# One transfer per expert, and gathers that skip empty rows, in a routed-expert kernel

## What is computed

```python
h = tok_ref(x, W, b, g1, b1, g2, b2)       # layer norm, 1024 -> 512, layer norm
h = h + attn_ref(layernorm(h), w_gate, g_gate, w_down, g_down)   # quantised gated MLP, width 1408
h = h + ffn_ref(layernorm(h), router_w, w_gate, w_up, w_down)

def ffn_ref(x, router_w, w_gate, w_up, w_down):     # 32 experts, 8 for each token, width 192
    probs = softmax(x @ router_w.T)
    rw, sel = top_k(probs, 8)
    rw = rw / sum(rw)
    for e in range(32):
        w_e = sum(where(sel == e, rw, 0))
        acc += (silu(x @ wg[e]) * (x @ wu[e])) @ wd[e] * w_e[:, None]
```

## Time and profile before

| | |
|---|---|
| median of 3 runs | 308.67 us (306.58 to 308.88) |
| profiled execution | 307.58 us |
| its span | 305.8 us |
| first gather issued | 103.33 us |
| first tile's rows turned | 107.06 us |
| last tile's down product ends | 279.7 us |
| last scatter issued | 283.06 us |
| mean DMA rate over the span | 280 GB/s |
| mean granted TensorE clock | 0.977 of full speed |

### The profile page before, as it was taken

How to read it: one execution, slowest core, us unless ns; L and a number is a source line. 1 busy time by engine, 2 the same in 40 slices (tenths; PEclk the granted TensorE clock), 3 DMA queues, 4 the chain that set the end, 5 groups by cost and what they waited for, 6 DMA issues and landing times.

```text
span 305.8 us, 3907 instructions
## 1 busy us (share of the span) xinstructions
PE 279.5 (91%) x1159; PEld 147.4 (48%) x1159; DVE 151.0 (49%) x446; ACT 125.1 (41%) x213; POOL 126.4 (41%) x130
## 2 busy tenths in 40 slices
PE   4899999779999889999999999999989999949991
PEld 1435444455557355655465556555645554533231
DVE  2648999995988523343523333323323322303364
ACT  2347998999974221332133213321322232211101
POOL 4062211976521422246435643464355446443310
PEclk9999999999998699999999999999999999997997
DMA  7999999503998298799999999999999999974883
GB/s 251 332 424 417 381 405 309 189 0 120 336 316 281 52 294 292 259 269 331 341 316 313 352 327 313 323 327 312 310 342 335 301 316 337 324 171 65 162 217 124
DMA packets 27798, 85.51 MB, mean 280 GB/s; under 512 B 4209, under 2 KB 4337, under 8 KB 26785
## 3 DMA queue, kind: packets, MB, share of 16 engines
q1 hardware_dynamic: 19760, 64.78, 61.0%
q0 software_dynamic: 7488, 18.42, 25.2%
q10 hardware_dynamic: 530, 2.08, 2.6%
HBM read 72.34 MB, written 12.92 MB: 279 GB/s over the span
## 4 chain that ended last, share of the span: by engine, by line
PE 39%; DVE 18%; DMA 17%; issue 8%; POOL 4%; ACT 3%; POOLq 0%; DVEq 0%; ACTq 0%
PE ps L1163 17%; DMA scrap<-token_rows,idx 9%; PE ps L1192 7%; DMA sum<-w_t,add_idx 5%; PE ps L1184 4%; PE ps L1195 4%; DMA ring<-sum 3%; DVE big L1443 2%; POOL sum L647 2%; DVE stats L1327 2%; PE ps L1050 2%; DVE raw L1449 2%; PE ps L1217 1%; PE ps L1147 1%; DVE hit L1625 1%
## 5 line engine op out<-in xcount | busy, mean ns | idle before, releaser
L633 POOL DMA_INDIRECT scrap<-token_rows,idx x36 | 35.9, 996 | 83.2 <-DVE idx L1628 46.8
L647 POOL DMA_INDIRECT sum<-w_t,add_idx x32 | 51.3, 1604 | 28.1 <-issue 11.5
L866 ACT ACTIVATE w_t<-ps 128x512 f32<-128x512 f32 x36 | 21.4, 597 | 85.0 <-PE ps L1184 84.8
L1644 DVE COPY w_t<-ps 128x256 f32<-128x256 f32 x34 | 14.4, 425 | 58.8 <-PE ps L1220 45.5
L1639 DVE SCALAR_TENSOR_TENSOR w_t<-ps,scrap,w_t 128x192 f32<-128x192 f32 x32 | 13.2, 413 | 57.1 <-issue 47.3
L871 ACT ACTIVATE w_t<-ps 128x192 f32<-128x192 f32 x34 | 11.2, 330 | 55.9 <-PE ps L1163 50.7
L1163 PE MATMUL ps<-ring,w_t 128*128 128x384 f32 x96 | 33.1, 487 | 0.7 <-ACT w_t L866 0.7
L1184 PE MATMUL ps<-ident,scrap 128*128 128x128 f32 x144 | 24.2, 292 | 10.1 <-DMA scrap<-token_rows,idx 6.6
L555 POOL TENSOR_TENSOR root_out<-root_in,minus_half 112x1 f32<-112x1 f32 x20 | 13.1, 654 | 46.3 <-DVE root_in L1344 46.2
L954 PE MATMUL ps<-raw,last 128*112 128x512 f32 x64 | 31.1, 639 | 0.0
L1163 PE MATMUL ps<-big,w_t 128*128 128x384 f32 x88 | 30.2, 486 | 0.0
(11 more groups left out here) (214 smaller groups left out, 470.6 us busy)
## 6 DMA issues: line engine op xcount, KB each, us to landing
big<-in_ffn_gate_up SPq DMA_DIRECT2D x15, 768.0 KB
ring<-in_ffn_gate_up SPq DMA_DIRECT2D x13, 768.0 KB
raw<-in_ffn_gate_up SPq DMA_DIRECT2D x6, 768.0 KB
last<-in_ffn_gate_up SPq DMA_DIRECT2D x6, 768.0 KB
big<-in_ffn_w_down SPq DMA_DIRECT2D x15, 256.0 KB
ring<-in_ffn_w_down SPq DMA_DIRECT2D x13, 256.0 KB
big<-in_mlp_w_in SPq DMA_DIRECT2D x2, 1536.0 KB, 17.7
big<-in_mlp_w_in SPq DMA_DIRECT2D x2, 1280.0 KB, 20.2
```

What stands on the lines that cost most here:

```text
L633: nc.gpsimd.indirect_dma_start(got[:, got_at(s), :], None, rows_dram[:, :], bass.IndirectOffsetOnAxis(ap=idx[:, s:s + 1], axis=0)).then_in ...
L647: nc.gpsimd.indirect_dma_start(acc_dram[m.two][:, :], bass.IndirectOffsetOnAxis(ap=add_idx[:, m.eight:m.eight + 1], axis=0), y[:, m.four, ...
L866: nc.scalar.activation(x_t[:, m.two, :, :], bank(2 + m.two).rearrange("p (c t) -> p c t", c=4), ACT.Copy).then_inc(xt_ready, 1)
L1644: nc.vector.tensor_copy(h_t[:, m.two, :, :], bank(6)[:, 0:2 * P].rearrange("p (c t) -> p c t", c=2)).then_inc(ht_ready, 1)
```

## The change

1. The weights of an expert come from one DRAM tensor `ffn` of 128 rows of 2560 numbers: gate and up, down rows 0 to 127, and in the last 512 columns the down rest. For even experts these columns hold the rest of the expert itself in partitions 0 to 63 and that of the next expert in 64 to 127. So an even expert is one transfer of 2560 columns, and an odd one a transfer of 2048 columns; `down_two` takes the rest of both from the even slot (`pair_rest_of`).
2. As an even slot holds something of both tiles, its load waits for the down products of both, and an odd slot's for its own; the separate wait on gate-up goes. `ld_dn` is gone: PE waits for `ld_gu` alone. The lists' loads keep a second, small transfer (`ld_rest`).
3. The tokens now are rows 0 to 447 of the DRAM tensors, and the spare rows 448 to 575. An empty place gets row 448 + p. All gathers but the first eight have a bound of 447: row numbers over it are skipped, and the buffer keeps what it held. Scatters still add 128 rows.
4. Experts 10 and 11 are still loaded after the first turned rows.

```diff
-    def down_loaded(self, u):
-        return 32 * self.k + 32 * ((NE + 4 * self.i + u) // R + 1)
+    def rest_loaded(self):
+        return 16 * self.k + 16
...
+        def pair_rest_of(n):
+
+            return slots[n - n % 2][rest_rows(n), WG + D:WCOLS]
...
-            def load_gate_up(e, n):
-                sp.dma_start(slots[n][:, 0:WG], we_gate_up[e, :, :]).then_inc(ld_gu[n], 16)
-
-            def load_down(e, n):
-                sp.dma_start(down_of(n), we_down[e, 0:P, :]).then_inc(ld_dn[n], 16)
-                sp.dma_start(down_rest_of(n), we_down[e, P:IE, :]).then_inc(ld_dn[n], 16)
-
             def load_expert(t):
-                load_gate_up(t, t)
-                load_down(t, t)
+
+                n, cols = t % R, WCOLS if t % 2 == 0 else WG + D
+                sp.dma_start(slots[n][:, 0:cols], ffn[t, :, 0:cols]).then_inc(ld_gu[n], 16)
+
+            def load_picked(e, n):
+
+                sp.dma_start(slots[n][:, 0:WG + D], ffn[e, :, 0:WG + D]).then_inc(ld_gu[n], 16)
+                sp.dma_start(down_rest_of(n), ffn[e, 0:IB, WG + D:WCOLS]).then_inc(ld_rest[n], 16)
...
             for t in range(R, NE):
-                sp.wait_ge(gu_done, t - R + 1)
-                load_gate_up(t, t % R)
-                sp.wait_ge(y_done, t - R + 1)
-                load_down(t, t % R)
+                sp.wait_ge(y_done, t - R + (1 if t % 2 else 2))
+                load_expert(t)
...
-                    sp.wait_ge(gu_done, R * k + (NE - R + n + 1))
-                    load_gate_up(bass.ds(e, 1), s)
                     sp.wait_ge(y_done, R * k + (NE - R + n + 1))
-                    load_down(bass.ds(e, 1), s)
+                    load_picked(bass.ds(e, 1), s)
...
-                nc.gpsimd.indirect_dma_start(got[:, got_at(s), :], None, rows_dram[:, :],
-                                             bass.IndirectOffsetOnAxis(ap=idx[:, s:s + 1], axis=0)
-                                             ).then_inc(ld_got[s], 16)
+                rows_ = bass.IndirectOffsetOnAxis(ap=idx[:, s:s + 1], axis=0)
+                if isinstance(m, Tile) and m.t < 8:
+                    nc.gpsimd.indirect_dma_start(got[:, got_at(s), :], None, rows_dram[:, :], rows_).then_inc(ld_got[s], 16)
+                else:
+                    nc.gpsimd.indirect_dma_start(got[:, got_at(s), :], None, rows_dram[:, :], rows_, bounds_check=TOK - 1,
+                                                 oob_is_err=False).then_inc(ld_got[s], 16)
...
                 for m in (Tile(t), Tile(t + 1)):
                     pe.wait_ge(ht_ready, m.upto())
-                    pe.wait_ge(ld_dn[m.slot], 2 * m.loaded())
...
-                nc.vector.tensor_scalar(idx[:, s:s + 1], idx_f[:, s:s + 1], iota_p[:, 0:1], None, ALU.max).then_inc(idx_ready, 1)
+                nc.vector.tensor_scalar(idx[:, s:s + 1], idx_f[:, s:s + 1], no_row[:, 0:1], None, ALU.add).then_inc(idx_ready, 1)
```

More of the change, by code:

```diff
@@ L104, in pairs_of, with program @@
         yield k, n_pairs
-def program(nc, x, w_tok, vecs, gb1, w_in, w_down, g_down, w_router, we_gate_up, we_down, out):
+def program(nc, x, w_tok, vecs, gb1, w_in, w_down, g_down, w_router, ffn, out):
     rows_dram = nc.dram_tensor("token_rows", (ROWS, ROW), F32).ap()
@@ L240, in program @@
         token = sb("token", [128, TOK], F16)
-        iota_p = sb("iota_p", [128, 1], F32)
+        no_row = sb("no_row", [128, 1], F32)
         iota_p2 = sb("iota_p2", [128, 1], F32)
@@ L315, in program @@
         ld_gu = [sem(f"ld_gu{n}") for n in range(R)]
-        ld_dn = [sem(f"ld_dn{n}") for n in range(R)]
+        ld_rest = [sem(f"ld_rest{n}") for n in range(R)]
         ld_got = [sem(f"ld_got{n}") for n in range(8)]
@@ L420, in program @@
         x_v = x.rearrange("(p g) k -> p g k", g=NG)
-        rows_v = rows_dram[P:ROWS, :].rearrange("(p g) r -> p g r", g=NG)
-        acc_v = [acc[P:ROWS, :].rearrange("(p g) d -> p g d", g=NG) for acc in acc_dram]
+        rows_v = rows_dram[0:TOK, :].rearrange("(p g) r -> p g r", g=NG)
+        acc_v = [acc[0:TOK, :].rearrange("(p g) d -> p g d", g=NG) for acc in acc_dram]
         def bcast(v, n):
@@ L460, in _ @@
             sp.wait_ge(consts, 1)
[L461 removed]
+            sp.dma_start(rows_dram[TOK:ROWS, :], zeros[:, :]).then_inc(rows_out, 16)
             for n in range(2):
[L463 removed]
+                sp.dma_start(acc_dram[n][TOK:ROWS, :], zeros[:, 0:D]).then_inc(sums_ready, 16)
             for n in range(2):
                 for g in range(NG):
[L466 to L477 removed]
+                    sp.dma_start(acc_dram[n][g * G:(g + 1) * G, :], zeros[0:G, 0:D]).then_inc(sums_ready, 16)
+            def load_expert(t):
+                n, cols = t % R, WCOLS if t % 2 == 0 else WG + D
[3 more added lines that the diff above has]
+                sp.dma_start(down_rest_of(n), ffn[e, 0:IB, WG + D:WCOLS]).then_inc(ld_rest[n], 16)
             sp.wait_ge(t1_done, NG)
@@ L584, in routing_consts @@
                 for t, pattern, base, mult in ((iota_e, [[0, 1]], 0, 1), (iota_e16, [[0, 1]], 0, 1), (iota_t, [[1, NL]], 0, 0),
-                                               (token, [[1, NG], [NG, G]], P, 0),
-                                               (iota_p, [[0, 1]], 0, 1), (iota_p2, [[0, 1]], 0, 2)):
+                                               (token, [[1, NG], [NG, G]], -TOK, -1),
+                                               (no_row, [[0, 1]], TOK, 1), (iota_p2, [[0, 1]], 0, 2)):
                     nc.gpsimd.iota(t[:, :], pattern=pattern, base=base, channel_multiplier=mult,
@@ L1194, in down_two @@
                     rows_ = rest_rows(m.slot)
-                    nc.tensor.matmul(bank(4 + m.two), h_t[rows_, m.two, 1, :], down_rest_of(m.slot), start=False, stop=True
+                    nc.tensor.matmul(bank(4 + m.two), h_t[rows_, m.two, 1, :], pair_rest_of(m.slot), start=False, stop=True
                                      ).then_inc(y_done, 1)
@@ L1206, in down_lists @@
                         if c == 0:
-                            pe.wait_ge(ld_dn[n], m.down_loaded(u))
+                            pe.wait_ge(ld_rest[n], m.rest_loaded())
                             nc.tensor.matmul(bank(4 + m.two)[rows_, :], h_t[:, m.two, 0, rows_], down_of(n), start=True, stop=False)
@@ L1765, in laid_out @@
     import numpy as np
+    rest = np.zeros((NE, P, D), we_down.dtype)
+    rest[:, 0:IB] = we_down[:, P:IE]
+    rest[0::2, IB:P] = we_down[1::2, P:IE]
     return {
@@ L1775, in laid_out @@
         "in_router_w": w_router.T.reshape(DC, 128, NE).transpose(1, 0, 2).reshape(128, DC * NE),
-        "in_ffn_gate_up": np.concatenate([w.reshape(NE, P, 4 * IE) for w in (we_gate, we_up)], axis=2),
-        "in_ffn_w_down": we_down,
+        "in_ffn": np.concatenate([w.reshape(NE, P, 4 * IE) for w in (we_gate, we_up)] + [we_down[:, 0:P], rest], axis=2),
     }
```

## The result

The changed kernel took 317.17 us (median of 4 runs, 314.41 to 317.86) against 307.62 (306.16 to 308.88) for the kernel before beside it. The ratio is 1.0295, 95% interval 1.0209 to 1.0382: 3% slower, where 302.1 us was forecast. The profiled execution took 317.86 us with a span of 315.9.

A forecast was written before the change was run, and what follows sets the result against it. PE, busy 91% of the span, was taken as the bound, so only its waits and the tail counted: list gather 3.4 + clock 1.4 + earlier waits 1.0 + tail 0.8 = 6.6 us, from 308.67 to 302.1; range 299.5 to 307.2.

The forecast's parts named there:

- The scatter in the stream: Expert stage: a scatter issued while weights stream takes 7.5 us, between 9.22 and 5.41.
- 93% forecast for the two queues: DMA queues, 170 to 190 us: weights 54% plus gathers and scatters 39%, against 105.5% before.
- 418 GB/s for the new rows: Weight stream: the new long rows flow at 418 GB/s while busy, against 348 for the old mix.
- The share of 54%: Weight queue q1, 170 to 190 us: busy share falls from 63.5% to 54%.
- The rival of the long packets: Expert stage: long weight packets lengthen scatters to 10.8 us, pairs to 11.7, bounding the kernel; 319 us, chance 0.08.
- Pairs take 10.2 us, PE-bound: Expert stage, 117 to 219 us: PE is full at 10.2 us a pair, so DMA work meanwhile is hidden.
- Later issue at nothing: Gate-up loads of the expert stage: issuing them up to one pair or 10 us later costs nothing.
- The bound: Gathers of tiles 8 to 31 and lists: empty rows left out, q0's share falls from 42% to 39%.
- The last list gather: End of expert stage: takes 5.0 us, lands at 270.8 instead of 274.2, 3.4 us gained.
- POOL's own time per gather: Issuing a bounded gather on POOL: 0.98 us may rise by 0 to 1 us, taken as 0.1.
- the 1.4 us of clock: Four matmuls at L1192 before the lists: a shorter PE wait keeps the clock up, 1.4 us gained.
- The tail: After the expert stage: empty gathers no longer share the engines with the accumulator read, 0.8 us gained.

The follow-up runs named there:

- e1: The changed kernel with every gather unbounded again, the rest of the change kept: 320.28 us.
- e9: The changed kernel with scatters dealt over four accumulators, two of them neither zeroed nor added, so half of the experts' sum is left out: 308.81 us, ratio 1.0055.
- e10: The changed kernel, but SP sends a pair's weights only when the odd tile's scatter then under way has landed: 320.45 us, ratio 1.0429.
- e4: The kernel before with only the later issue of gate-up, after the down product of its slot's pair: 308.79 us, ratio 1.0075.
- e2: The kernel before with only the bounded gathers and the new numbering of rows: 301.51 us, ratio 0.9851.

## Why the prediction was wrong

- **The scatter in the stream, put at 7.5 us, is the step that failed.** It took 10.3 us for odd tiles and 6.1 for even ones. I reasoned with a mean: less use of the engines (93% forecast for the two queues, 96.7% measured from 170 to 190 us), so every transfer shorter. The mean of the two did fall, from 9.0 to 8.2. But the chain from scatter to scatter is set by the longer kind, and long rows made the kinds unequal.
- **418 GB/s for the new rows: wrong.** They ran at 352 beside the gathers (363 to 376 in e1, e9 and e10), the old mix at 348. The stretch of 418 in the earlier trace rows had no gathers beside it. The best rate beside gathers was 392, with 4 and 5 KB rows. The share of 54% was met (53.5) for another reason, the slower pairs.
- **The rival of the long packets had the mechanism in the main, and its total with some luck.** It had 0.35 us for a weight packet (0.357 measured), 10.8 us for a scatter (10.3, single ones to 11.5), 11.7 us for a pair (11.47) and 319 us in all (317.17). But it made all scatters longer and not the odd ones alone, and its total is eight pairs longer by 1.5 us each, where nine longer by 1.17 were found. I gave it 0.08, on the argument that the weights are through in 6 of 10 us and meet scatters only in part. From 140 to 250 us the loads landed 7.7 to 12.4 us after their issue. The rows could have told otherwise: after the change the loads leave on the pair's down product, and so do the pair's scatters. It also began at 143 us, not at 190. The Trainium skill's rule of turns by packets (DMA: Bandwidth & Descriptors, Queues, rings and completion order) agrees in its direction with the series of row lengths, 7.1 to 10.3 us. No run shows the turns themselves, and one weight packet for each scatter row is not what was counted: 290 packets of q1 beside 452 of q0 with long rows, 712 beside 413 with short ones.
- **"Pairs take 10.2 us, PE-bound" was 0.3 us off.** With short rows a pair takes 9.86 us in the middle of the stage and 9.95 to 10.00 in the mean. The rest was already scatters of 9.2 us and more, each with 0.9 us to the next (from about 190 us on): the old kernel stood at the edge, which is 9.0 us of scatter (9.86 − 0.9), near the rival's 9.3.
- **Later issue at nothing: 2.3 us instead** (e4, with the old rows).
- **The bound, right in size.** The last list gather took 4.17 us in the changed kernel and under 4.41 in e2, forecast 5.0. POOL's own time per gather rose from 0.98 to 1.06 us, forecast 0.1. But in the changed kernel it went out at 281.55 and PE waited 3.61 us, since the scatters before it were late. So the 1.4 us of clock behind it didn't come back either: the four matmuls of L1193 there take 2.83 us, against 3.30 before and 1.9 forecast. In e2, where the scatters before it were not late, PE waited 1.86 us and the clock behind it stayed at 1.00.
- **The tail: right, and somewhat larger.** The last sums no longer wait for the accumulator. From the end of the last down product of a tile to the end of the span it is 24.7 us (315.9 − 291.2) against 26.1 (305.8 − 279.7), 1.4 less where 0.8 was forecast.

## What to carry to other kernels

A large transfer is more than its bytes. In this kernel the length of its rows went with the time that small transfers of another queue needed beside it, 7.1 to 10.3 us. Where a chain of such small transfers is near the bound, try cutting the large ones by columns over all 128 partitions (rows of 1 to 5 KB were alike here within the intervals), and don't cut by partitions. Before crediting a lower share of the DMA engines, look for the one transfer that others wait for and give it its worst case, not the mean.

## What I had not expected of the hardware

- A single transfer of 1.0 to 1.25 MB with rows of 8 and 10 KB had hardly a better rate beside the gathers (352 GB/s) than the mix of rows of 2 and 6 KB with a 64-partition piece (348), and a lower one than the same bytes in two pieces (392). The Trainium skill (SBUF — State Buffer, The DMA setup-cost knee) advises, for transfers that are bound by DMA, the largest single one over 128 partitions; here one took 317.17 us and four took 303.04, so for a stream that shares the engines the measurement goes against it.
- Weights in halves of 64 partitions brought the stream to 253 GB/s and the kernel to 359.63 us, the largest effect of all.
- Long rows don't make all scatters slower: in the changed kernel those of even tiles, sent some us ahead of the pair's loads, took 6.1 us, and those of odd tiles, sent with them or up to 3 us behind, 10.3. In e10, where both went out with or just ahead of the loads, both took over 10.
